# First pair's projection weights and first normalised tokens in small parts, and a transposed-probability copy moved between two low-part subtractions

## The chip, the cores and the metric

The kernel runs on one core of one Trainium2 chip. The metric is the device time of one execution in microseconds (us); lower is better. Three runs of the kernel before took 746.08, 747.19 and 747.55 us, median 747.19 us.

## The reference, cut to what matters

A decoder layer over x of shape (16, 128, 256), all in float32:

```
x = x + attn(layernorm(x), Wq, Wk, Wv, Wr)                     # 16 heads of 64, causal penalty -50
x = x + xattn(layernorm(x), ctx, ctx, w_q, w_k, w_v, w_o)      # 16 heads of 64, no mask
x = x + ffn(layernorm(x))                                      # shared SwiGLU + 8 experts, two chosen per token

attn:  q, k, v = x @ Wq, x @ Wk, x @ Wv                        # 256 -> 1024 columns each
       p = softmax(q k^T / 8 + mask);  out = (p v) @ Wr
```

## The kernel before, in words

**Precision.** A float32 matrix is split into a high part (rounded to the fast matmul type, by ScalarE) and a low part (the rest, by VectorE or GpSimd). `product` (L145 to L149) multiplies two such matrices in three matmuls: low by high, high by high, high by low, at L147, L148 and L149.

**Tiling.** The 2048 tokens are four groups of 512 (four sequences of 128). The 16 heads are eight pairs of two, so that a pair's q or k is a tile of 128 rows and 512 tokens. Two pairs make a duo; a group has four duos d = 0 to 3, self-attention has 16 duos and cross-attention 16 more, so that the attention is a pipeline of 32 duos. After it come the gating, the shared and the routed feed-forward. The order of every engine is written out by hand, and the engines meet at semaphores alone.

**A duo.** On TensorE (`duo` inside `attention_tensor`): the weighted values of the two pairs of the duo before last (`weighted_values`, L887, into the two banks of psW), the transposes of the first pair's probabilities of the duo before (`p_transposes(pe, 0)`, L873, into both banks of psT), the scores of this duo's two pairs (`scores`, L941, into psS and psA), the transposes of the second pair's probabilities (`p_transposes(pe, 1)`, again into psT), and then projections of q, k and v for what follows, and the output projection. In the last quarter of `scores(p, 1)` TensorE waits (`psT_free`) until both banks of psT have been copied out: bank 0 by ScalarE (`pT0_copy`, L580), bank 1 by VectorE (`pT1_copy`, L717). VectorE's order at the head of a duo is `oT_split_lo` of pair 0, `oT_split_lo` of pair 1 (L721: the low part of the weighted values, which needs ScalarE's high part, L584), then `pT1_copy`, then the row minima of the scores (L740). The output projection and the next user of each psW bank need the low parts.

**The start.** SP loads two of the first group's four token tiles (ScalarE's queue the other two) and then three weight pieces of 512 KB each, half the columns of Wq, Wk and Wv, into three slots of `stage` (`PIECES`, `load`). Every later piece waits until the piece in its slot has been split. TensorE runs 13 matmuls on the identity (`WARM`, L904), each of which shows as two records. VectorE takes the statistics and normalises the four tiles (L210); `first_z_transposes` (L243) transposes each tile into two banks, k = 1 and k = 0; ScalarE rounds each 512-token bank (`z_split_hi`, L251) and VectorE subtracts (`z_split_lo`, L257). ScalarE's order there is wq high (L337), z high, wk high, wv high; VectorE's is z rows, wq low (L341), z low, wk low, wv low. Then TensorE makes q and k of pair 0 (`q_or_k`), a quarter of v (`v_project`), the scores of pair 0 (`scores(0, 0)`), and q and k of pair 1.

Of the kernel before, what the change touches and what calls it, by code (L numbers as in the profile page):

```python
# [20 lines left out]
F32 = mybir.dt.float32  # L21
F32R = mybir.dt.float32r
ACT = mybir.ActivationFunctionType
# [3 lines left out]
P = 128  # L27
# [19 lines left out]
CHUNK = KT * INNER  # L47
WARM = 13
STAGES = 3
# [12 lines left out]
def build(nc, x, ctxT, wq, wk, wv, wr, xq, xk, xv, xr, w1, win, wout, w2, wgate, bgate, out):  # L62
    ctx = ExitStack()
    with ctx:
        def sem(name):
            return ctx.enter_context(nc.semaphore(name))
# [34 lines left out]
        rstd_seen, z_centred = sem("rstd_seen"), sem("z_centred")  # L101
        first_eps, first_rstd = sem("first_eps"), sem("first_rstd")
        zT_mm, z_hi, z_lo = sem("zT_mm"), sem("z_hi"), sem("z_lo")
        qk_mm, q_copied, k_copied = sem("qk_mm"), sem("q_copied"), sem("k_copied")
# [100 lines left out]

        def first_rows(dve):
            for half, known in ((FIRST, first_rstd), (SECOND, rstd_done)):
                dve.wait_ge(known, 1)
                for t in range(half.start, half.stop):
                    nc.vector.tensor_scalar(z[:, t, :], row_tile(0, t), mv[:, t, 0:1], rstd[:, t:t + 1],  # L210
                                            ALU.subtract, ALU.mult).then_inc(z_done, 1)
# [15 lines left out]
        Z_IN_S = ((1, psS[:, 0, :]), (0, psS[:, 1, :]))  # L227
        Z_FIRST = ((1, psW[:, 0, :]), (0, psT[:, 0, :]))
        Z_IN_A = ((1, psA[:, 0, :]), (0, psA[:, 1, :]))
# [8 lines left out]

        def first_z_transposes(pe, halves):
            for t in range(TPG):  # L240
                pe.wait_ge(z_done, t + 1)
                for k, bank in halves:
                    mm = nc.tensor.transpose(bank[:, t * P:(t + 1) * P], z[:, t, k * P:(k + 1) * P], ident[:])  # L243
                    if t == TPG - 1:
                        mm.then_inc(zT_mm, 1)

        def z_split_hi(act, g, halves, hi=None):
            hi = zhi if hi is None else hi
            for n, (k, bank) in enumerate(halves):
                act.wait_ge(zT_mm, g * KT + n + 1)  # L250
                nc.scalar.activation(hi[:, k, :], bank, ACT.Copy).then_inc(z_hi, 1)  # L251
# [43 lines left out]
        def token_half(pair, z_g, t, half, k):  # L295
# [12 lines left out]
        PIECES = [f"{w} {half}" for w, half in  # L308
                  (("wq", "lower"), ("wk", "lower"), ("wv", "lower"), ("wq", "upper"), ("wk", "upper"), ("wr", "lower"),
                   ("wv", "upper"), ("wr", "upper"),  # L310
# [74 lines left out]
        with att:  # L385
# [33 lines left out]
            pieces = [columns(Q, wq, lower, -SCALE), columns(K, wk, lower, 1.0), columns(V, wv, lower, 1.0),  # L419
                       columns(Q, wq, upper, -SCALE), columns(K, wk, upper, 1.0), pair_rows(wr, slice(0, HP)),  # L420
# [165 lines left out]
            def attention_scalar(act):  # L586
# [137 lines left out]
            def attention_vector(dve):  # L724
# [5 lines left out]
                def first_lo(n):  # L730
                    weights_lo(dve, n, pieces[n][2], pieces[n][1], pieces[n][3])
# [15 lines left out]
                def duo(G, d, after, causal=True, depth=2, sub=0):  # L747
# [152 lines left out]
            def attention_tensor(pe):  # L900
# [956 lines left out]
```

## Time and profile before

| | |
|---|---|
| three runs, us | 746.08, 747.19, 747.55 |
| profiled execution: its time, us | 745.39 |
| profiled execution: its span, us | 743.7 |
| granted TensorE clock, mean of the span | 1.000 |
| TensorE matmul busy | 735.5 us (99% of the span) |
| VectorE busy | 460.3 us (62%) |
| ScalarE busy | 443.2 us (60%) |
| GpSimd busy | 309.3 us (42%) |

The span runs from the first to the last instruction; the execution's own time is 1.7 us more. PE is TensorE's matmuls, PEld its weight loads, DVE VectorE, ACT ScalarE, POOL GpSimd, SPq and ACTq the DMA issues of these engines. L12 is a line of the kernel. Matmuls are pipelined, so that a record's duration overlaps the next record: what one takes of TensorE's time is read from start to start.

### The profile page before, as it was taken

The page shows a single profiled execution, that of the slowest core. Times are in us where ns is not written, and L with a number is a line of the kernel's source. Part 1 is how long each engine was busy: PE and PEld are TensorE (multiplying, and loading weights), DVE is VectorE, ACT ScalarE, POOL GpSimd, SP SyncE. Part 2 cuts the span into 40 slices and gives each one's busy share as a digit, 9 for nine tenths or more (in the row PEclk, how much of TensorE's full clock was granted, in tenths as well). Part 3 has the DMA queues.
Part 4 walks back from the last instruction along what each step waited for, and adds up shares of the span by engine and source line. Part 5 has one row for each costly group of instructions (what it writes and reads, how often), then busy time and mean ns, then how long its engine had stood idle before and what let it go on. Part 6 is the DMA issues. An engine that isn't in the chain of part 4 may idle for free.

```text
span 743.7 us, 17776 instructions
## 1 busy us (share of the span) xinstructions
PE 735.5 (99%) x6371; PEld 643.2 (86%) x6371; DVE 460.3 (62%) x947; ACT 443.2 (60%) x1469; POOL 309.3 (42%) x336
## 2 busy tenths in 40 slices
PE   7999999999999999999999999999999999999998
PEld 6888888888988888888888889888887889999987
DVE  6776677766766875554466456455777746444277
ACT  4876666666656678766566666657744534555322
POOL 2656225222523556463244236323760772555400
PEclk9999999999999999999999999999999999999999
DMA  7599800000000013000000000300150455767272
GB/s 235 175 372 192 263 1 0 0 0 0 0 0 0 30 37 107 2 26 5 1 0 28 0 0 1 112 0 2 30 226 1 185 200 179 240 207 213 69 270 67
DMA packets 35418, 64.68 MB, mean 87 GB/s; under 512 B 7940, under 2 KB 14596, under 8 KB 34788
## 3 DMA queue, kind: packets, MB, share of 16 engines
q1 hardware_dynamic: 30644, 50.17, 21.8%
q0 software_dynamic: 4432, 13.54, 4.8%
q8 instruction: 33, 0.54, 0.3%
q10 hardware_dynamic: 288, 0.26, 0.1%
q14 instruction: 21, 0.17, 0.1%
HBM read 38.06 MB, written 30.09 MB: 92 GB/s over the span
## 4 chain that ended last, share of the span: by engine, by line
PE 98%; ACT 1%; DVE 0%; POOL 0%; issue 0%; POOLq 0%; DVEq 0%
PE psW L147 15%; PE psW L149 14%; PE psW L148 14%; PE psW L887 8%; PE psT L873 5%; PE psT L147 4%; PE psT L148 4%; PE psT L149 4%; PE psA L941 4%; PE psS L941 4%; PE psS L147 4%; PE psS L148 3%; PE psS L149 3%; PE psA L149 2%; PE psA L148 2%; PE psA L147 2%
## 5 line engine op out<-in xcount | busy, mean ns | idle before, releaser
L506 POOL TENSOR_TENSOR prob<-prob,rsum 128x512 f32<-128x512 f32 x128 | 134.8, 1055 | 287.9 <-DVE rsum L745 287.8
L609 ACT ACTIVATE prob<-psA,nmin 128x128 f32<-128x128 f32 x256 | 91.8, 384 | 1.3
L609 ACT ACTIVATE prob<-psS,nmin 128x128 f32<-128x128 f32 x256 | 90.4, 376 | 1.9 <-DVE nmin L740 1.9
L584 ACT ACTIVATE oT_hi<-psW 128x512 fp32r<-128x512 f32 x63 | 37.7, 598 | 88.2 <-PE psW L887 88.2
L580 ACT ACTIVATE pT<-psT 128x512 f32<-128x512 f32 x64 | 38.3, 598 | 54.3 <-PE psT L873 53.4
L745 DVE RECIPROCAL rsum<-psums 128x4 f32<-128x4 f32 x128 | 21.9, 171 | 71.4 <-ACT prob L609 71.2
L721 DVE TENSOR_TENSOR oT_lo<-psW,oT_hi 128x512 fp32r<-128x512 f32 x63 | 43.5, 691 | 31.4 <-ACT oT_hi L584 31.0
L887 PE MATMUL psW<-pT,v 128*64 128x128 f32 x1008 | 62.3, 276 | 0.0
L728 DVE COPY kt<-psW 128x512 f32<-128x512 f32 x57 | 39.3, 689 | 36.7 <-PE psW L149 36.7
L887 PEld LDWEIGHTS psW<-pT,v 128*64 128x64 f32 x1008 | 54.4, 137 | 6.6 <-issue 3.1
L609 ACT ACTIVATION_READ_ACCUMULATOR prob<-psA,nmin 128x1 f32 x256 | 57.5, 225 | 0.0
L1241 POOL DMA_INDIRECT yt<-z,probs x39 | 37.9, 972 | 46.8 <-ACT z L1323 32.6
L609 ACT ACTIVATION_READ_ACCUMULATOR prob<-psS,nmin 128x1 f32 x256 | 55.6, 217 | 0.0
L147 PE MATMUL psW<-zlo,wq_hi 128*128 128x512 f32 x128 | 53.2, 416 | 1.4 <-DVE zlo L257 1.4
L149 PE MATMUL psW<-zhi,wq_lo 128*128 128x512 f32 x128 | 50.6, 395 | 0.0
L148 PE MATMUL psW<-zhi,wq_hi 128*128 128x512 f32 x128 | 50.3, 393 | 0.0
L595 ACT ACTIVATE q<-psW 128x512 f32<-128x512 f32 x64 | 38.9, 608 | 17.2 <-PE psW L149 16.9
L147 PE MATMUL psW<-wo_lo,oT_hi 128*128 128x256 f32 x168 | 48.9, 291 | 0.0
L148 PE MATMUL psW<-wo_hi,oT_hi 128*128 128x256 f32 x168 | 46.8, 279 | 0.0
L149 PE MATMUL psW<-wo_hi,oT_lo 128*128 128x256 f32 x168 | 46.8, 278 | 0.0
L873 PE MATMUL psT<-ident,prob 64*128 64x64 f32 x1024 | 44.9, 225 | 0.0
L873 PEld LDWEIGHTS psT<-ident,prob 64*128 64x128 f32 x1024 | 39.5, 139 | 5.8 <-issue 5.8
(378 smaller groups left out, 2194.7 us busy)
## 6 DMA issues: line engine op xcount, KB each, us to landing
stage<-hs SPq DMA_DIRECT2D x39, 257.0 KB, 2.9
hs<-empty SPq DMA_DIRECT2D x1, 9984.0 KB, 35.2
w_lo<-w_raw SPq DMA_DIRECT2D x4, 1024.0 KB, 8.1
w_hi<-yt SPq DMA_DIRECT2D x4, 1024.0 KB, 9.4
stage<-ctxT SPq DMA_DIRECT2D x4, 512.0 KB, 4.3
xres<-x SPq DMA_DIRECT2D x3, 512.0 KB, 6.9
out<-xres SPq DMA_DIRECT2D x12, 128.0 KB, 2.0
stage<-wq SPq DMA_DIRECT2D x2, 512.0 KB, 4.0
```

The source lines that it names most:

```text
L147: nc.tensor.matmul(o, lh, rl, start=start, stop=False, **kw)
L148: nc.tensor.matmul(o, lh, rh, start=False, stop=False, **kw)
L149: return nc.tensor.matmul(o, ll, rh, start=False, stop=stop, **kw)
L506: nc.gpsimd.tensor_tensor(prob[i][:, r, :], prob[i][:, r, :], rsum[i][:, r].unsqueeze(2).broadcast_to([P, TPG, P]), ALU.mult).then_inc(pro ...
L580: nc.scalar.activation(flat(pT[i][:, 0, :, :]), psT[:, 0, :], ACT.Copy).then_inc(pT0_copied, 1)
L595: nc.scalar.activation(q[i][:], psW[:, Q, :], ACT.Copy).then_inc(q_copied, 1)
L609: e = nc.scalar.activation(prob[i][:, n, :], flat(psX[i][:])[:, n * P:(n + 1) * P], ACT.Exp, bias=nmin[i][:, n:n + 1], scale=-1.0, accum_o ...
L721: nc.vector.tensor_tensor(flat(oT[i][1][:]), bank, flat(oT[i][0][:]).bitcast(F32), ALU.subtract).then_inc(oT_lo, 1)
L728: nc.vector.tensor_copy(kt[i][:], bank).then_inc(k_copied, 1)
L873: mm = nc.tensor.transpose(psT[:, half, c], prob[i][r, n, :], ident[r, r])
L887: mm = nc.tensor.matmul(bank[r, keys].rearrange("p (a q) -> p a q", a=2), v[:, b, c], pT[i][:, :, h * TPG + b, :], start=True, stop=True, ...
L941: mm = nc.tensor.matmul(psX[i][:, h, c], q[i][r, c], kt[i][r, c], start=True, stop=True, skip_group_check=True)
```

## The change

Four things change at the start, and one in every duo.

- The first pair's 128 columns of Wq and of Wk are pieces of their own (128 KB each), loaded ahead of all others into a spare part of `stage` and split with their own semaphores. The other 384 columns of each lower half follow after wv, and TensorE waits for them (`wk lower`) ahead of q and k of pair 1.
- The first z is transposed, rounded and subtracted by halves of 256 tokens: tokens of tiles 0 and 1 in psW and psT, tokens of tiles 2 and 3 in the two banks of psS. q of pair 0 is computed in two halves of 256 tokens, k of pair 0 in one.
- VectorE's low part of the first wq columns stands between the rows of tiles 0 and 1 and those of tiles 2 and 3.
- `WARM` is 10 instead of 13.
- In each duo that has all three, VectorE's `pT1_copy` stands between the two `oT_split_lo`.

```diff
-WARM = 13
+WARM = 10
-        def first_rows(dve):
+        def first_rows(dve, between):
             for half, known in ((FIRST, first_rstd), (SECOND, rstd_done)):
+                if half is SECOND:
+                    between()
-        Z_FIRST = ((1, psW[:, 0, :]), (0, psT[:, 0, :]))
+        Z_FIRST_A = ((1, psW[:, 0, :]), (0, psT[:, 0, :]))
+        Z_FIRST_B = ((1, psS[:, 0, :]), (0, psS[:, 1, :]))
+        TOKENS_A, TOKENS_B = slice(0, GT // 2), slice(GT // 2, GT)
...
+                for k, bank in Z_FIRST_A if t < TPG // 2 else Z_FIRST_B:
                     mm = nc.tensor.transpose(bank[:, t * P:(t + 1) * P], z[:, t, k * P:(k + 1) * P], ident[:])
+                    if t == TPG // 2 - 1:
+                        mm.then_inc(first_zT, 1)
...
+        def first_split_hi(act, halves, tokens, transposed, signal):
+            for n, (k, bank) in enumerate(halves):
+                act.wait_ge(transposed, n + 1)
+                nc.scalar.activation(zhi[:, k, tokens], bank[:, tokens], ACT.Copy).then_inc(signal, 1)
+
+        def first_split_lo(dve, halves, tokens, copied, signal):
+            for n, (k, bank) in enumerate(halves):
+                dve.wait_ge(copied, n + 1)
+                nc.vector.tensor_tensor(zlo[:, k, tokens], bank[:, tokens], zhi[:, k, tokens].bitcast(F32),
+                                        ALU.subtract).then_inc(signal, 1)
...
-                  (("wq", "lower"), ("wk", "lower"), ("wv", "lower"), ("wq", "upper"), ...
+                  (("wv", "lower"), ("wq", "lower"), ("wk", "lower"), ("wq", "upper"), ...
+            FIRST_PAIR, OTHER_PAIRS = slice(0, P), slice(P, HC)
+            first_pieces = [columns(Q, wq, FIRST_PAIR, -SCALE), columns(K, wk, FIRST_PAIR, 1.0)]
+            first_stage = [stage[:, n + 1, CHUNK // 2:CHUNK // 2 + KT * P].rearrange("p (a b) -> p a b", a=KT) for n in range(2)]
...
+                for n in range(2):
+                    sp.dma_start(first_stage[n], first_pieces[n][0]).then_inc(first_in[n], 16)
                 for n in range(STAGES):
                     load(sp, n, pieces[n][0])
...  (ScalarE)
-                first_hi(Q)
-                z_split_hi(act, 0, Z_FIRST)
-                first_hi(K)
-                first_hi(V)
+                first_pair_hi(Q)
+                first_split_hi(act, Z_FIRST_A, TOKENS_A, first_zT, first_z_hi)
+                first_split_hi(act, Z_FIRST_B, TOKENS_B, zT_mm, z_hi)
+                first_pair_hi(K)
+                first_hi(PIECES.index("wv lower"))
                 q_copy(0, 0)
+                first_hi(PIECES.index("wq lower"))
+                first_hi(PIECES.index("wk lower"))
                 v_copy(0, 0, 0, psT[:, 1, :])
...  (VectorE, in a duo)
                         oT_split_lo(dve, p - 4, 0, psW[:, 0, :])
-                        oT_split_lo(dve, p - 4, 1, psW[:, 1, :])
                     if depth > 0:
                         pT1_copy(dve, p - 2, 0)
+                    if depth > 1:
+                        oT_split_lo(dve, p - 4, 1, psW[:, 1, :])
...  (VectorE, the start)
-                first_rows(dve)
-                first_lo(Q)
-                z_split_lo(dve, 0, Z_FIRST)
-                first_lo(K)
-                first_lo(V)
+                first_rows(dve, lambda: first_pair_lo(Q))
+                first_split_lo(dve, Z_FIRST_A, TOKENS_A, first_z_hi, first_z_lo)
+                first_split_lo(dve, Z_FIRST_B, TOKENS_B, z_hi, z_lo)
+                first_pair_lo(K)
+                first_lo(PIECES.index("wv lower"))
                 k_copy(0, 0)
+                first_lo(PIECES.index("wq lower"))
+                first_lo(PIECES.index("wk lower"))
...  (TensorE)
-                first_z_transposes(pe, Z_FIRST)
-                q_or_k(0, Q, 0, None, 0)
-                q_or_k(0, K, 0, None, None)
+                first_z_transposes(pe)
+                pe.wait_ge(first_w_lo, 1)
+                first_product(Q, TOKENS_A, first_z_lo, True, False)
+                first_product(Q, TOKENS_B, z_lo, False, True)
+                pe.wait_ge(first_w_lo, 2)
+                first_product(K, slice(0, GT), None, True, True)
                 wait_lo(pe, "wv lower")
                 v_project(0, 0, 0, psT[:, 1, :])
                 scores(0, 0, free=False)
+                wait_lo(pe, "wk lower")
                 q_or_k(0, Q, 1, None, None)
```

`first_pair_hi(n)` and `first_pair_lo(n)` are one ScalarE and one VectorE instruction on 128x256 numbers, as L337 and L341 are on 128x1024. `first_product` is `product` for each k (1, then 0) on the tokens given, into psW, with a wait for each k's low part where `known` is given.

## Rows read from the trace of the kernel before

**Rows 1.** Page, part 4: share of the span in the chain that ended last.

```profile
PE 98%; ACT 1%; DVE 0%; POOL 0%; issue 0%; POOLq 0%; DVEq 0%
```

**Rows 2.** Waits of PE: waiting, releaser, us in total, times, longest.

```profile
PE psW L147 <- DVE zlo L257: 1.4, 1, 1.4
```

**Rows 3.** Timeline of PE, 2 to 8 us, then 6.95 to 7.45: start, us, what.

```profile
2.44 5.17 PE L904 MATMUL psA<-ident 128*128 128x128 f32 x26 [2.44 <-POOL mask L499]
...
6.78 0.83 PE L904 MATMUL psA<-ident 128*128 128x128 f32 x6
```

**Rows 4.** Timeline of all engines, 0 to 22 us.

```profile
6.40 1.06 ACT L337 ACTIVATE wq_hi<-stage 128x1024 fp32r<-128x1024 f32 x1 [3.39 <-DMA stage<-wq]
6.72 0.75 DVE L210 TENSOR_SCALAR z<-xres,mv,rstd 128x256 f32<-128x256 f32 x2 [0.27 <-POOL rstd L193]
...
8.41 0.60 ACT L251 ACTIVATE zhi<-psW 128x512 fp32r<-128x512 f32 x1 [0.96 <-PE psW L243]
...
10.48 1.23 DVE L341 SCALAR_TENSOR_TENSOR wk_lo<-stage,wk_hi 128x1024 fp32r<-128x1024 f32 x1
...
11.76 0.50 PE L147 MATMUL psW<-zlo,wk_hi 128*128 128x512 f32 x1 [0.25 <-DVE wk_lo L341]
...
13.26 0.39 PE L147 MATMUL psT<-wv_lo,zhi 128*128 128x512 f32 x1
...
15.84 0.50 PE L147 MATMUL psW<-zlo,wq_hi 128*128 128x512 f32 x1
...
21.10 1.11 ACT L337 ACTIVATE wq_hi<-stage 128x1024 fp32r<-128x1024 f32 x1
```

**Rows 5.** DMA issues between 1.6 and 2.75 us: KB each, us from issue to landing.

```profile
stage<-wq SPq DMA_DIRECT2D x1, 512.0 KB, 4.7
xres<-x SPq DMA_DIRECT2D x1, 128.0 KB, 3.0
...
stage<-wv SPq DMA_DIRECT2D x1, 512.0 KB, 6.3
```

**Rows 6.** Timeline of PE in a duo of the middle, 306 to 309.4 us.

```profile
307.67 1.14 PE L941 MATMUL psA<-kt,q 64*128 64x128 f32 x16
308.61 0.69 PE L873 MATMUL psT<-ident,prob 64*128 64x64 f32 x16
309.23 0.50 PE L147 MATMUL psW<-zlo,wq_hi 128*128 128x512 f32 x1
```

**Rows 7.** Timeline of DVE in the same duo.

```profile
306.04 0.69 DVE L721 TENSOR_TENSOR oT_lo<-psW,oT_hi 128x512 fp32r<-128x512 f32 x1 [0.97 <-ACT oT_hi L584]
306.92 0.69 DVE L721 TENSOR_TENSOR oT_lo<-psW,oT_hi 128x512 fp32r<-128x512 f32 x1 [0.18 <-ACT oT_hi L584]
307.53 0.68 DVE L717 COPY pT<-psT 128x512 f32<-128x512 f32 x1
```

**Rows 8.** Timeline of PEld there, 308.305 to 308.31 us: the one load in flight.

```profile
308.28 0.18 PEld L941 LDWEIGHTS psA<-kt,q 64*128 64x128 f32 x1
```

**Rows 9.** Timeline of ACT there.

```profile
306.92 0.60 ACT L580 ACTIVATE pT<-psT 128x512 f32<-128x512 f32 x1
...
310.92 0.60 ACT L595 ACTIVATE q<-psW 128x512 f32<-128x512 f32 x1 [0.33 <-PE psW L149]
```

**Rows 10.** Timelines of PE and DVE in the second duo, 27 to 30.2 us.

```profile
28.57 1.06 PE L941 MATMUL psA<-kt,q 64*128 64x128 f32 x16
29.46 0.66 PE L873 MATMUL psT<-ident,prob 64*128 64x64 f32 x16
30.05 0.50 PE L147 MATMUL psW<-zlo,wq_hi 128*128 128x512 f32 x1
...
27.85 0.69 DVE L717 COPY pT<-psT 128x512 f32<-128x512 f32 x1
```

**Rows 11.** Timeline of PE, third and last duo: the block in psA.

```profile
42.19 1.12 PE L941 MATMUL psA<-kt,q 64*128 64x128 f32 x16
...
521.63 1.14 PE L941 MATMUL psA<-kt,q 64*128 64x128 f32 x16
```

More of the change, by code:

```diff
@@ L102, in build @@
         first_eps, first_rstd = sem("first_eps"), sem("first_rstd")
+        first_in = [sem(f"first_in{n}") for n in range(2)]
+        first_w_hi, first_w_lo = sem("first_w_hi"), sem("first_w_lo")
+        first_zT, first_z_hi, first_z_lo = sem("first_zT"), sem("first_z_hi"), sem("first_z_lo")
         zT_mm, z_hi, z_lo = sem("zT_mm"), sem("z_hi"), sem("z_lo")
@@ L237, in z_transposes, with first_z_transposes @@
                 mm.then_inc(zT_mm, 1)
-        def first_z_transposes(pe, halves):
+        def first_z_transposes(pe):
             for t in range(TPG):
                 pe.wait_ge(z_done, t + 1)
-                for k, bank in halves:
+                for k, bank in Z_FIRST_A if t < TPG // 2 else Z_FIRST_B:
                     mm = nc.tensor.transpose(bank[:, t * P:(t + 1) * P], z[:, t, k * P:(k + 1) * P], ident[:])
+                    if t == TPG // 2 - 1:
+                        mm.then_inc(first_zT, 1)
                     if t == TPG - 1:
                         mm.then_inc(zT_mm, 1)
+        def first_split_hi(act, halves, tokens, transposed, signal):
[7 more added lines that the diff above has]
+                                        ALU.subtract).then_inc(signal, 1)
         def z_split_hi(act, g, halves, hi=None):
@@ L308, in build @@
         PIECES = [f"{w} {half}" for w, half in
-                  (("wq", "lower"), ("wk", "lower"), ("wv", "lower"), ("wq", "upper"), ("wk", "upper"), ("wr", "lower"),
+                  (("wv", "lower"), ("wq", "lower"), ("wk", "lower"), ("wq", "upper"), ("wk", "upper"), ("wr", "lower"),
                    ("wv", "upper"), ("wr", "upper"),
@@ L417, in pair_rows @@
                 return (k_rows(src)[:, r, :], wo_hi[:, r, :], wo_lo[:, r, :], 1.0)
-            pieces = [columns(Q, wq, lower, -SCALE), columns(K, wk, lower, 1.0), columns(V, wv, lower, 1.0),
+            FIRST_PAIR, OTHER_PAIRS = slice(0, P), slice(P, HC)
+            first_pieces = [columns(Q, wq, FIRST_PAIR, -SCALE), columns(K, wk, FIRST_PAIR, 1.0)]
+            first_stage = [stage[:, n + 1, CHUNK // 2:CHUNK // 2 + KT * P].rearrange("p (a b) -> p a b", a=KT) for n in range(2)]
+            pieces = [columns(V, wv, lower, 1.0), columns(Q, wq, OTHER_PAIRS, -SCALE), columns(K, wk, OTHER_PAIRS, 1.0),
                        columns(Q, wq, upper, -SCALE), columns(K, wk, upper, 1.0), pair_rows(wr, slice(0, HP)),
@@ L684, in first_hi, with first_pair_hi @@
                     weights_hi(act, n, pieces[n][1], pieces[n][3])
-                first_hi(Q)
-                z_split_hi(act, 0, Z_FIRST)
-                first_hi(K)
-                first_hi(V)
+                def first_pair_hi(n):
+                    act.wait_ge(first_in[n], 16)
+                    nc.scalar.activation(first_pieces[n][1], first_stage[n], ACT.Copy,
+                                         scale=first_pieces[n][3]).then_inc(first_w_hi, 1)
+                first_pair_hi(Q)
[3 more added lines that the diff above has]
+                first_hi(PIECES.index("wv lower"))
                 q_copy(0, 0)
+                first_hi(PIECES.index("wq lower"))
+                first_hi(PIECES.index("wk lower"))
                 v_copy(0, 0, 0, psT[:, 1, :])
@@ L840, in attention_vector, with first_pair_lo @@
                 first_stats(dve)
-                first_rows(dve)
-                first_lo(Q)
-                z_split_lo(dve, 0, Z_FIRST)
-                first_lo(K)
-                first_lo(V)
+                def first_pair_lo(n):
+                    dve.wait_ge(first_w_hi, n + 1)
+                    nc.vector.scalar_tensor_tensor(first_pieces[n][2], first_stage[n], first_pieces[n][3],
+                                                   first_pieces[n][1].bitcast(F32), ALU.mult, ALU.subtract).then_inc(first_w_lo, 1)
+                first_rows(dve, lambda: first_pair_lo(Q))
[3 more added lines that the diff above has]
+                first_lo(PIECES.index("wv lower"))
                 k_copy(0, 0)
+                first_lo(PIECES.index("wq lower"))
+                first_lo(PIECES.index("wk lower"))
                 for d in range(PEEL):
@@ L1046, in duo, with first_product @@
                             projections(1, True, first_copied)
-                first_z_transposes(pe, Z_FIRST)
-                q_or_k(0, Q, 0, None, 0)
-                q_or_k(0, K, 0, None, None)
+                def first_product(n, tokens, known, start, stop):
+                    for i, k in enumerate((1, 0)):
+                        if known is not None:
+                            pe.wait_ge(known, i + 1)
+                        mm = product(psW[:, n, tokens], (wh[n][:, k, FIRST_PAIR], wl[n][:, k, FIRST_PAIR]),
+                                     (zhi[:, k, tokens], zlo[:, k, tokens]), start and i == 0, stop and i == KT - 1,
+                                     skip_group_check=True)
+                    if stop:
+                        mm.then_inc(qk_mm, 1)
+                first_z_transposes(pe)
[4 more added lines that the diff above has]
+                first_product(K, slice(0, GT), None, True, True)
                 wait_lo(pe, "wv lower")
```

## The prediction

> **What bounds the kernel now.** I read the chain of waits first: 98% of the span is TensorE's work [rows 1]. So two questions are left: where TensorE stands still, and where its work is slower than it need be. The table of waits answers the first for the large stops: 1.4 us ahead of q's first matmul, for the low part of z, and at 11.76 us a short one of 0.25 for the low part of wk; it names none in a duo [rows 2, 4]. The start's timeline then shows what TensorE is fed by: the transposes wait behind the warm-up, ScalarE takes the two banks of z and then wk, VectorE the low parts one after another [rows 3, 4]. For stops too short for the table I compared the same piece of TensorE's program from start to start in two duos. In the second duo, scores in psA to next transposes to q's first matmul take 29.46 - 28.57 = 0.89 and 30.05 - 29.46 = 0.59 us, together 1.48 [rows 10]. In a middle duo the same instructions take 0.94 and 0.62, together 1.56 [rows 6]. The matmul rows name no cause, the weight loads do: in the middle duo the load for the last quarter of the scores starts at 308.28 [rows 8], 0.07 after VectorE's copy of psT's second bank ends (307.53 + 0.68 = 308.21) [rows 7], and TensorE waits for this very copy there (`psT_free`). In the second duo that copy ended at 28.54, before the scores began [rows 10]. So TensorE does wait in a steady duo, by 0.05 us; the other 0.03 comes in the transposes behind it, which I read as the two heads' records running out of step after the stop. Of 32 such blocks the first two lie ahead of the pattern; the third to the last are 30, and their own durations (1.12 and 1.14 against 1.06) carry its mark at both ends [rows 10, 11].
>
> **The reordered copy.** It removes nothing and adds nothing; it puts `pT1_copy` ahead of the second low part. VectorE is free at 306.04 + 0.61 = 306.65 (two such instructions in a row start 0.61 apart [rows 7]), and psT is ready when ScalarE's copy of the other bank starts, 306.92 [rows 9]. The copy then runs 306.92 to 307.60, and ScalarE's ends at 307.52, both well ahead of 308.22, where the load would come unhindered. The stop goes. Per duo 1.56 - 1.48 = 0.08 us, by 30 duos 2.3 us; I take 2.2, as the third duo's stop is smaller. The ends: nothing, if the stop is something else; 30 x 0.08 = 2.4 at the most. What is late next: the second low part, now 307.53 to 308.22, is wanted by TensorE only in the projections behind q, whose six matmuls start at 309.23, so more than 2 us later [rows 6]; it is covered by the scores in psA, the transposes and q. The row minima queued behind it start at the same time as before, since the two instructions have only changed places, and the 0.18 us that VectorE idled for ScalarE now goes into waiting for the transposes [rows 7]. ScalarE is fed by TensorE again right after (0.33 us idle before the copy of q at 310.92 [rows 9]), so its work moves forward with TensorE's and doesn't hold the gain back. I price these at zero.
>
> **The start.** I follow the new order with rows' durations. Where the trace has no such size (128x256) I take 0.45 us on ScalarE and 0.42 on VectorE, estimates: z's rows of that size take (0.75 us for two that overlap, so 0.34 apart) [rows 4], and 128x512 takes 0.60 on ScalarE, 0.69 on VectorE [rows 4, 7]. Back to back I space them 0.34. Upper end: no gain over the 512 size, 0.60.
> - Warm-up: 26 records from 2.44 to 7.45, the last six 0.11 apart from 6.78, so the 20 before took 4.34 us, 0.217 each [rows 3]. Ten matmuls are these 20: the warm-up ends at 6.78, which is where the spacing falls to its fast value, the level of 2.4 GHz against 1.2. The transposes of tiles 0 and 1 (their rows are done before) follow at 6.78 to 7.22.
> - wq's first columns (128 KB, issued at 1.70 like wq before): between 3.0 us, as a token tile of this size, and 4.7, as the whole wq [rows 5], so landed between 4.7 and 6.4; I take 4.9, the nearer size. ScalarE's high part then lies beside the statistics, and VectorE's low part in the 0.27 us in which it idled before 6.72 [rows 4]: it starts at 6.45, the second rows 0.34 later at 6.79, which is 0.07 late, ending 7.54. Landed at 6.4, they would be 0.45 late.
> - z's high parts on ScalarE: 7.30, 7.64, and for the second half (transposes from 7.63) 7.98, 8.32 to 8.77. Low parts on VectorE: 7.78, 8.12, 8.46, 8.80 to 9.22. TensorE computes q in between; its last three short matmuls end at about 9.67. The high part of wk's first columns starts at 8.66, the low part at 9.14 to 9.57.
> - k: six matmuls from 9.67, ready for v at 11.1 (before: 11.76 to 13.26, 1.50 with its slow first one [rows 4]).
> - wv: high part 9.00 to 10.06 on ScalarE, low part 10.09 to 11.31 on VectorE (1.06 and 1.23 for this size [rows 4]). v starts at 11.36, 0.25 us after TensorE is free: this is the wait that takes the place of the 1.4. wv was issued at 2.69 and took 6.3 [rows 5], landed 8.99; now 256 KB stand ahead of it instead of 1 MB, so it should be there. Were it to land with the old delay it would just do.
> - v and the scores of pair 0 take what they took, 15.84 - 13.26 = 2.58 [rows 4]: TensorE is at pair 1 at 13.94. Its new wait there, for wk's other columns: VectorE copies k at 11.45 to 12.14, then two low parts of 128x768 (0.96 each, 1.23 x 3/4 and a little, spaced 0.88) to 13.90. Just in time, 13.95. Behind this wait q and k of pair 1 are queued and everything else of TensorE; behind VectorE's two low parts stands the mask of the first scores, which come at 14.0.
> So pair 1 starts at 13.95 instead of 15.84: 1.9 us. With 0.60 for each small ScalarE step (five of them ahead of wv, each 0.15 dearer, and the last low part behind) v starts at 12.1, and the gain is 1.1; with a ScalarE step of 0.38 it is 2.2. The later slots of `stage`: the upper wq is now issued after wv's low part at 11.3, and ScalarE takes it at 21.10 - 1.9 = 19.2 [rows 4], 7.9 us later, where pieces of its size landed in 4.7 to 6.3 [rows 5]. Hidden, and without that cover it would cost what the landing is late. SP's two added issues push its later ones back by some half a microsecond each, the pieces of wq, wk and the gate's weights among them; their cover is the 2 us between their landing (like wv's before, about 9.0) and their first use at 10.9 on ScalarE.
>
> **A rule of the skill against it.** The rise of TensorE's spacing comes at 6.6 to 6.8 us in this execution, with no reserve for a shorter warm-up [rows 3]. The Trainium skill ("TensorE: Matmul & The Clock Gate", section "What's actually happening") says that the array is throttled until activity releases it, and that how many matmuls run slow differs between runs of one kernel. By that rule some executions would enter q and k at half the clock. One trace can't show the spread; I make it the third case below.
>
> **Sum.** 745.39 - 1.9 - 2.2 = 741.3 us for the profiled execution; the runs' median lies 1.80 above that execution, so 743.1 for the runs.
>
> **Rivals.**
> A. *Both steps as above*: 743.1, own range 742.1 to 744.3 (start 1.1 to 2.2, duos 1.8 to 2.4, and half a microsecond of scatter, as the three runs show).
> B. *The duos give nothing.* For: 0.05 us is at the edge of what start times tell, and another wait, as ScalarE's copy of q before the output projection, could swallow it. Against: load and copy end keep 0.07 between them, and the second duo runs the same program without it. 747.19 - 1.9 = 745.3.
> C. *The start gives nothing, by the clock.* With the warm-up gone from 6.78 on, the pauses between the small q products leave TensorE less active than before, and the spacing stays at 0.217 per 128 two-pass columns until about 12. q's 12 short matmuls and k's 6 then cost twice 0.115 and twice 0.23, 1.4 us more each where they are not waiting; k would end at some 13.3, as before. 747.19 - 2.2 = 745.0.
> D. *Slower than before.* The same mechanism, lasting: with the low clock from 9.7 us on, each microsecond so spent costs half of one, all of it on the path. To eat 4.1 us it must last 8.2 us, to 18; to 24 it costs 7.1 against 4.1 won, 750.2. For: TensorE pauses more in this start than now. Against: it has no pause over 0.5 us from 8.2 on, while the old one paused 1.4 us before q [rows 2] and was fast after it (six matmuls of k in 1.50 [rows 4]).
> E. *No change*: both B and C, 747.2.
>
> **Chances.** A 0.68, B 0.12, C 0.14, D 0.03, E 0.03. The range for 8 in 10 reaches from 741.7 to 745.6, A with both its ends and the centres of B and C. About 0.2% (1.5 us) is what a measurement of this kernel can tell: faster means below 745.7. A lies there whole, B by some 0.6 of its cases, C by 0.75: 0.68 + 0.07 + 0.10 = 0.85. Same 0.12, slower 0.03.
>
> **What would show it.** Right: the psA block and its transposes take 1.48 us from start to start in all duos, and the weight load no longer follows VectorE's copy by 0.07; pair 1's q starts near 14.0; wv's low part ends at 11.3 and v starts right behind; warm-up records end at 6.8 with transposes 0.11 apart. Wrong: matmuls of k some 0.46 us apart (C, D); ScalarE idle for wv or for wq's first columns past 5 us (the pieces land late); a block still at 1.56 with the load behind another instruction's end (B); q of pair 1 later than 14.5 behind wk's low part.

## The result, and the profile after

The changed kernel took 741.66 us (median of six runs, 741.35 to 741.98); the kernel before, now in six runs, 747.26 us (746.08 to 748.93). The ratio is 0.9925, 95% interval 0.9913 to 0.9937: 5.6 us faster, where 4.1 was forecast, and 0.04 us below the range. The two profiled executions stand closer to the forecast than the medians do: 745.39 and 741.35 us, 4.04 apart, spans 743.7 and 739.6. So the reading falls into two parts: what the traces show of the 4.1 us, and where the other 1.5 are.

**The duos.** Timeline of PE in the same middle duo of the changed kernel (start, us, what), to be read against [rows 6]:

```profile
304.78 1.06 PE L981 MATMUL psA<-kt,q 64*128 64x128 f32 x16
305.67 0.66 PE L913 MATMUL psT<-ident,prob 64*128 64x64 f32 x16
306.26 0.50 PE L150 MATMUL psW<-zlo,wq_hi 128*128 128x512 f32 x1
```

and of DVE, against [rows 7]:

```profile
303.16 0.69 DVE L753 TENSOR_TENSOR oT_lo<-psW,oT_hi 128x512 fp32r<-128x512 f32 x1 [0.97 <-ACT oT_hi L608]
304.06 0.69 DVE L749 COPY pT<-psT 128x512 f32<-128x512 f32 x1 [0.21 <-PE psT L913]
304.67 0.68 DVE L753 TENSOR_TENSOR oT_lo<-psW,oT_hi 128x512 fp32r<-128x512 f32 x1
```

Scores to q take 306.26 - 304.78 = 1.48 us, as in the second duo of before [rows 10], instead of 1.56, and the row's own duration is 1.06 instead of 1.14. The copy ends at 304.75, before TensorE's block in psA starts. VectorE's idle time has moved from the low part to the copy, as forecast. From pair 1's q to the last scores before took 522.50 - 15.84 = 506.66 us and after 518.32 - 14.31 = 504.01: 2.65 us for 30 duos.

**The start.** PE, ACT and DVE of the changed kernel, to be read against [rows 3, 4]:

```profile
2.44 4.63 PE L944 MATMUL psA<-ident 128*128 128x128 f32 x20 [2.44 <-POOL mask L523]
...
5.33 0.42 ACT L712 ACTIVATE wq_hi<-stage 128x256 fp32r<-128x256 f32 x1 [2.33 <-DMA stage<-wq]
...
6.20 0.42 DVE L876 SCALAR_TENSOR_TENSOR wq_lo<-stage,wq_hi 128x256 fp32r<-128x256 f32 x1
...
6.87 0.42 PE L250 MATMUL psW<-ident,z 128*128 128x128 f32 x1
7.08 0.42 PE L250 MATMUL psT<-ident,z 128*128 128x128 f32 x1
...
7.75 0.38 ACT L259 ACTIVATE zhi<-psW 128x256 fp32r<-128x256 f32 x1 [2.01 <-PE psW L250]
...
8.74 0.36 PE L150 MATMUL psW<-zlo,wq_hi 128*128 128x256 f32 x1 [0.31 <-DVE zlo L264]
...
10.31 1.22 DVE L361 SCALAR_TENSOR_TENSOR wv_lo<-stage,wv_hi 128x1024 fp32r<-128x1024 f32 x1 [0.39 <-ACT wv_hi L357]
...
13.30 0.95 DVE L361 SCALAR_TENSOR_TENSOR wk_lo<-stage,wk_hi 128x768 fp32r<-128x768 f32 x1
...
14.31 0.50 PE L150 MATMUL psW<-zlo,wq_hi 128*128 128x512 f32 x1
```

The chain is the one that was written down, 0.36 us later at its end: pair 1's q at 14.31 for 13.95, against 15.84 before. The delay comes in at one place. The first transposes are 0.21 us apart, not 0.11: TensorE was still at its lower clock, as rival C had it, but for one microsecond only (the granted clock rose at 7.94 us, in the first trace of before at 6.67). From there everything is late: z's high part at 7.75 (7.30 forecast), wv's low part ends at 11.53 (11.31), wk's other columns at 14.25 (13.90).

Behind the last scores both traces take nearly the same time (221.16 and 221.26 us, to the end of the span). 1.53 + 2.65 - 0.10 = 4.08: the traces are accounted for.

### The profile page after: what moved, and what is told of

Same layout as the page of the kernel before. It is cut to its first block, busy times and chain, and to the rows that moved or that the text cites. A ratio compares the mean times of both kernels' runs of the same rounds, so it can differ in the third digit from the quotient of the medians.

```text
span 739.6 us, 17762 instructions
## 1 busy us (share of the span) xinstructions
PE 732.7 (99%) x6371; PEld 641.1 (87%) x6371; DVE 459.8 (62%) x951; ACT 443.6 (60%) x1473; POOL 309.3 (42%) x336
## 4 chain that ended last, share of the span: by engine, by line
PE 98%; ACT 0%; DVE 0%; POOL 0%; issue 0%; POOLq 0%; DVEq 0%
PE psW L150 15%; PE psW L152 14%; PE psW L151 14%; PE psW L927 8%; PE psT L913 5%; PE psT L150 4%; PE psT L152 4%; PE psT L151 4%; PE psS L981 4%; PE psA L981 4%; PE psS L150 4%; PE psS L152 3%; PE psS L151 3%; PE psA L152 2%; PE psA L151 2%; PE psA L150 2%
## 5 line engine op out<-in xcount | busy, mean ns | idle before, releaser
L150 PE MATMUL psW<-zlo,wq_hi 128*128 128x512 f32 (+1 forms) x130 | 53.5, 412 | 0.3 <-DVE zlo L264 0.3
L152 PE MATMUL psW<-zhi,wq_lo 128*128 128x512 f32 (+1 forms) x130 | 50.8, 391 | 0.0
L151 PE MATMUL psW<-zhi,wq_hi 128*128 128x512 f32 (+1 forms) x130 | 50.6, 389 | 0.0
L749 DVE COPY pT<-psT 128x512 f32<-128x512 f32 x64 | 43.9, 685 | 6.6 <-PE psT L913 6.4
L772 DVE TENSOR_REDUCE nmin<-psA 128x4 f32<-128x512 f32 x64 | 43.9, 687 | 1.1
```

Source lines behind the costliest of these rows:

```text
L150: nc.tensor.matmul(o, lh, rl, start=start, stop=False, **kw)
L151: nc.tensor.matmul(o, lh, rh, start=False, stop=False, **kw)
L152: return nc.tensor.matmul(o, ll, rh, start=False, stop=stop, **kw)
L749: nc.vector.tensor_copy(flat(pT[i][:, 1, :, :]), psT[:, 1, :]).then_inc(pT1_copied, 1)
L772: nc.vector.tensor_reduce(nmin[i][:, h * TPG:(h + 1) * TPG], sc, AX.X, ALU.min).then_inc(min_done, 1)
```

## The experiments

Kernels of one batch ran on one chip with runs of the kernel before beside them. In three of the four batches every kernel, the one before too, has a stop of some 19 us near 600 us (below), so that times are compared within a batch. Its length differs from execution to execution: behind the last scores the twelve traces with the stop take 238.7 to 241.1 us, the six without it 221.1 to 221.4. So batches 1, 2 and 4 carry up to 2.4 us of scatter that no part of this change makes.

**Batch 1: the parts alone.** Before was at 766.50 us there.

E1, the reorder alone (the diff's part in the duos, put into the kernel before). 

> The kernel before with one edit: in each duo VectorE's copy of the transposes stands between the two low parts. Theory T1 (the duos' stops are all that the reorder takes, 30 x 0.08 us, and what the runs moved beyond the traces' 4.1 us belongs to them, as their length differs from run to run): median 3.5 to 4.0 us under before, runs within 0.7 us of each other as the changed kernel's are. Rival T2 (the part beyond 4.1 us belongs to the start): 2.2 to 2.4 us under before, runs scattered over 1.5 to 3 us as before's. Rival T3 (the part beyond is only that the profiled execution of before was an unusually quick one): 2.4 us under before whatever the scatter. Trace: score block and transposes 1.48 us from start to start in every duo.

 Measured: 763.73 us (760.64 to 765.48), ratio 0.9964 (0.9949 to 0.9978), 2.8 us less (1.7 to 3.9 by the interval, so that this run alone doesn't tell T1 from T2 and T3). Trace: 305.75 to 307.23 from scores to q, 1.48 us.

E2, the start alone:

```diff
                         oT_split_lo(dve, p - 4, 0, psW[:, 0, :])
+                        oT_split_lo(dve, p - 4, 1, psW[:, 1, :])
                     if depth > 0:
                         pT1_copy(dve, p - 2, 0)
-                    if depth > 1:
-                        oT_split_lo(dve, p - 4, 1, psW[:, 1, :])
```

> The changed kernel with the old order in the duos: the low parts first, then the copy. T1: 1.5 us under before (pair 1's q at 14.3 instead of 15.8 us), runs as scattered as before's. T2: 3 us under before, runs tight. T3: 1.6 us under before. Trace: the stop is back, 1.56 us from start to start in every duo, the weight load 0.07 us behind the copy's end.

 Measured: 763.36 us (761.87 to 766.02), ratio 0.9962 (0.9949 to 0.9975), 2.9 us less. Trace: q of pair 1 at 14.03; the stop is back (1.56 us from scores to q in the steady duos).

The parts add up (0.9964 x 0.9962 = 0.9926, the whole change 0.9925). The reorder gives what its trace says. The start gives 2.9 us, nearly twice what the first pair of traces says, though its interval reaches down to 1.9: T1, which gave the missing part to the duos, fell, and T2 stands, save that its other sign failed: neither kernel's runs drew together here (E2's reach over 4.2 us). The stop near 600 us hides part of what that sign could show.

E3, the kernel before again. 

> The kernel before, unchanged, for a second trace of it: what differs between two executions of the same program. T1: time within 0.2% of before's median; if this execution is longer than 745.39 us, the excess stands in the duos, as longer stops in the last quarter of the scores in psA. T2: the excess stands ahead of pair 1's q (15.84 us in the first trace), as a later rise of TensorE's spacing. T3: no excess, some 745.4 us.

 Measured: 765.57 us (764.87 to 768.40), ratio 0.9991 (0.9978 to 1.0005). Trace: pair 1's q at 15.79, so no excess at the start; but from there to the last scores 507.72 us instead of 506.66. The 1.05 us stand in the cross-attention loop's output projection. Timeline of PE and ACT in one of its duos, the first execution of before:

```profile
366.65 0.62 ACT L595 ACTIVATE q<-psW 128x512 f32<-128x512 f32 x1
...
367.39 0.32 PE L147 MATMUL psW<-wo_lo,oT_hi 128*128 128x256 f32 x1
...
368.79 0.28 PE L147 MATMUL psT<-wo_lo,oT_hi 128*128 128x256 f32 x1
```

and in the second, with PEld's row:

```profile
366.82 0.62 ACT L595 ACTIVATE q<-psW 128x512 f32<-128x512 f32 x1
...
367.49 0.19 PEld L147 LDWEIGHTS psW<-wo_lo,oT_hi 128*128 128x128 f32 x1 [0.21 <-ACT q L595]
...
367.55 0.32 PE L147 MATMUL psW<-wo_lo,oT_hi 128*128 128x256 f32 x1
...
369.01 0.28 PE L147 MATMUL psT<-wo_lo,oT_hi 128*128 128x256 f32 x1
```

The weight load follows the end of ScalarE's copy of q (367.44) by 0.05 us, and the block takes 1.40 us in the one execution and 1.46 in the other, in all ten duos of the loop's inside; the block behind it 1.45 and 1.50. The loop settles into one of two rhythms and keeps it. But the wait is not what differs. In both executions the load starts 0.05 us behind the copy's end, and the first matmul's step is 0.156 and 0.162 us; each of the 22 steps behind it takes 0.1134 us in the one and 0.1177 in the other, at the full granted clock in both. What spaces them differently isn't shown.

The rhythm has to be kept apart when the duos are priced. From pair 1's q to the last scores, with the old order in the duos, three traces in the short rhythm take 506.9 us on average (first, E10, E16) and four in the long one 507.7 (E2, E3, E11, E14); with the new order 504.0 in two (first, E5) and 504.8 in four (E1, E4, E12, E13). In either rhythm the reordered copy is worth 2.9 us, as E1's runs have it.

E4, 13 warm-up matmuls in the changed kernel (`WARM = 13`). 

> The changed kernel with 13 warm-up matmuls instead of 10. If the clock rises by the time since the first matmul, as before (6.7 us), the 6 more records cost 0.11 each and the transposes of tiles 0 and 1 come at 7.45 with fast spacing, tiles 2 and 3 right behind: pair 1's q within 0.2 us of the changed kernel's 14.31. If the rise comes at a time that changes from execution to execution, whatever the warm-up, then records up to it are 0.21 apart and the transposes start at 7.45 to 8.0: up to 0.5 us slower. Time against the changed kernel: 0 to +0.5 us.

 Measured: 762.38 us (761.39 to 763.49), ratio 0.9949 (0.9932 to 0.9967); the changed kernel's own ratio is 0.9923 to 0.9925, so it is slower than that by some 2 us, with intervals that overlap, where at most 0.5 was expected. Trace: q of pair 1 at 14.84, 0.5 us later than with 10; it is also in the long rhythm. The shorter warm-up is worth half a microsecond in the trace, and no trace shows the loss that it risked.

**Batch 2: other orders.** Before was at 765.97 us.

E5, the changed kernel again. 

> The changed kernel, unchanged, beside the kernel before on this chip. Theory T1 (the traces are right, duos 2.7 us and start 1.5 us; the rest of the 5.6 us is scatter of the kernel before alone): 4.0 to 4.5 us under before. Rival T4 (the kernel before really loses 1.5 us more in most executions than in its profiled one, and the changed kernel doesn't): 5.2 to 6 us under before again, and its own runs within 1 us.

 Measured: 760.34 us (760.07 to 760.82), ratio 0.9923 (0.991 to 0.9937): 5.6 us again. T4 stands: the kernel before is usually slower than its profiled execution, the changed one isn't.

E6, ScalarE's copy of q one exponential earlier:

```diff
-                        exps(p, 1, range(2, 6 if depth > 1 else 4))
+                        exps(p, 1, range(2, 5 if depth > 1 else 4))
                         q_copy(p + 2, 1)
-                        exps(p, 1, range(6 if depth > 1 else 4, 8))
+                        exps(p, 1, range(5 if depth > 1 else 4, 8))
```

> The changed kernel with ScalarE's copy of the second pair's q (of the next duo) one exponential earlier in duos 1 and 2. In the changed kernel's trace the weight load of the output projection starts 0.05 us after that copy ends, in 22 duos, where its twelve matmuls take 1.44 to 1.46 us against 12 x 0.115 = 1.38. If that wait is real: 1.3 to 2 us under the changed kernel, the block at 1.38. If the 0.06 is only the change of tile shape: no change within 0.3 us.

 Measured: 757.97 us (757.71 to 759.57), ratio to before 0.9897 (0.988 to 0.9913), 2.4 us under the changed kernel (1.3 to 2 were expected). The same two rows, 1.37 us apart and without the longer first one:

```profile
362.51 0.28 PE L150 MATMUL psW<-wo_lo,oT_hi 128*128 128x256 f32 x1
...
363.88 0.28 PE L150 MATMUL psT<-wo_lo,oT_hi 128*128 128x256 f32 x1
```

The wait was real: the first step is 0.113 us instead of 0.156. The long rhythm doesn't show either: all twelve blocks from the loop on take 1.36 us, with steps of 0.1134, here and in the two other traces with this edit (E9, E15).

E7, the second low part later still:

```diff
-                    if depth > 1:
-                        oT_split_lo(dve, p - 4, 1, psW[:, 1, :])
                     minima(p, 0, 0, causal)
                     minima(p, 0, 1, causal)
+                    if depth > 1:
+                        oT_split_lo(dve, p - 4, 1, psW[:, 1, :])
```

> The changed kernel with the second low part behind both row minima, 1.3 us later again. If the low part has the 2 us of cover that the prediction gave it: same time as the changed kernel within 0.5 us. If TensorE's projections behind q wait for it: up to 1.3 us a duo, 30 us in all.

 Measured: 771.01 us (770.01 to 772.19), ratio 1.0056 (1.004 to 1.0071): 10.7 us over the changed kernel. PE's waits:

```profile
PE psW L150 <- DVE oT_lo L753: 6.6, 14, 0.5
```

The expected 1.3 us was wrong: the low part now ends 3.0 us later in a masked duo (the mask doubles what stands ahead of it), and TensorE waits for it in 14 duos, 0.5 us each by the table. From start to start such a duo loses 0.73 us, 10.2 in all. The 16 duos of cross-attention, where the low part comes 1.5 us later, take 246.8 us against 245.9, and the 0.9 is no more than the long rhythm, in which this trace is. So the cover was there as the prediction had it: in the changed kernel's trace the low part ends at 74.70 and the first projection that wants it starts at 77.09, 2.4 us.

E8, the copy behind both low parts and the first minima. 

> The changed kernel with VectorE's copy of the transposes behind both low parts and behind the first row minima. If TensorE waits for the end of this copy alone, each of the 30 duos loses what the copy comes later beyond the moment it is wanted: 0.6 us later than in the kernel before, in 14 unmasked duos (one instruction of minima), 1.3 in 15 masked ones (mask and minima): 26 to 32 us over the changed kernel. If something else ends the wait: under 5 us.

 Measured: 802.17 us (two runs), ratio 1.0467: 41.8 us over the changed kernel. Timelines of an unmasked duo, PE and DVE:

```profile
385.97 0.49 PE L983 MATMUL psA<-kt,q 64*128 64x128 f32 x4 [0.75 <-issue]
...
384.58 0.69 DVE L772 TENSOR_REDUCE nmin<-psS 128x4 f32<-128x512 f32 x1 [0.25 <-PE psS L983]
385.19 0.68 DVE L749 COPY pT<-psT 128x512 f32<-128x512 f32 x1
```

The last quarter of the scores starts at 385.97, 0.10 after the copy's end at 385.87. TensorE's wait for this instruction is shown. My size (26 to 32) was short by a third: I left out that the minima can't start before the scores in psS are done (the 0.25 us of idle time), so that the block takes 1.88 us unmasked and 2.62 masked, for 0.89.

**Batch 3: the kernel before's own scatter.** Before was at 747.69 us (22 runs, 746.47 to 749.85), without the stop at 600.

E9, the same earlier copy of q in the kernel before. 

> The kernel before with ScalarE's copy of q one exponential earlier in duos 1 and 2, nothing else. Theory T5 (in the cross-attention loop the wait of the output projection for this copy settles into one of two lengths, 1.40 or 1.46 us for its block and 1.45 or 1.50 for the next, 1.05 us over the loop; the kernel before is mostly in the long one, the changed kernel in the short one, and its first profiled execution was in the short one): the wait goes, so the gain over before is the 22 waits and the 1.05 us, 2.5 to 3.5 us, and the runs draw together. Without T5 the gain is as over the changed kernel, 2 to 2.5 us, and the scatter stays.

 Measured: 745.62 us (744.85 to 746.72), ratio 0.9967 (0.9957 to 0.9978), 2.1 us less, under the 2.5 that T5 asked for. All blocks of the loop at 1.36 us again; the runs reach over 1.9 us for 3.4, with half as many of them. In its trace wq's first piece is split only at 7.56:

```profile
7.56 1.06 ACT L337 ACTIVATE wq_hi<-stage 128x1024 fp32r<-128x1024 f32 x1 [4.55 <-DMA stage<-wq]
...
9.02 0.60 ACT L251 ACTIVATE zhi<-psW 128x512 fp32r<-128x512 f32 x1 [0.40 <-PE psW L243]
...
16.43 0.50 PE L147 MATMUL psW<-zlo,wq_hi 128*128 128x512 f32 x1
```

E10, 10 warm-up matmuls in the kernel before (`WARM = 10`). 

> The kernel before with 10 warm-up matmuls instead of 13. The transposes of the first z then start near 7.5 us, where the last rows are ready, instead of 7.45 to 8.0. T1 and T5: pair 1's q at 15.6 to 15.9 as before, time within 0.5 us of before, unless the order of events at the start moves the loop into its other length, 1 us less. Rival T6 (the warm-up is what the start's gain comes from): 1 to 1.5 us under before.

 Measured: 748.41 us (745.11 to 750.69), ratio 1.0009 (0.9996 to 1.0022). T6 fell: the shorter warm-up alone gives nothing, though q of pair 1 is at 15.27 in its trace, earlier than the 15.6 expected.

E11, before a third time. 

> The kernel before once more, for a third trace. T5: output-projection blocks in the cross-attention loop at 1.46 us (long), as in the second trace. If it is at 1.40, the long one is not what most executions show, and T5 doesn't explain before's median.

 Measured: 749.71 us, one run, near the upper end of the batch; its trace holds a term that the first one doesn't show. ACT and PE, then the table of stretches (busy time and instructions of PE, PEld, DVE, ACT and POOL, granted clock, DMA share, GB/s):

```profile
8.54 1.06 ACT L337 ACTIVATE wq_hi<-stage 128x1024 fp32r<-128x1024 f32 x1 [5.54 <-DMA stage<-wq]
...
11.61 0.47 PE L147 MATMUL psW<-zlo,wq_hi 128*128 128x512 f32 x1 [3.42 <-DVE zlo L257]
...
18.69 0.50 PE L147 MATMUL psW<-zlo,wq_hi 128*128 128x512 f32 x1
```

```profile
10.00:12.00 2.00, 0.39 (x2) 0.38 (x3) 2.00 (x4) 2.00 (x4) 0.00 (x0) 1.00 0.06 16
...
13.00:16.00 3.00, 3.00 (x9) 2.18 (x8) 1.33 (x2) 0.60 (x1) 0.00 (x0) 0.50 0.71 254
```

The first 512 KB piece of wq landed 6.8 us after its issue, not 4.7. ScalarE's high parts of z are queued behind that of wq, so TensorE stood idle for 3.4 us, up to 11.61; 1.2 us after that its granted clock fell to the lower level, and k took 2.73 us instead of 1.50. Pair 1's q started 2.85 us later than in the first trace: 1.72 of it stand ahead of q's first matmul, the other 1.13 behind it, where the clock was low. The loop's rhythm was the long one.

E12, the changed kernel a third time. 

> The changed kernel once more, for a third trace. T5: output-projection blocks in the cross-attention loop at 1.40 us (short), as in the first two; pair 1's q at 14.0 to 14.5.

 Measured: 742.23 us. Pair 1's q at 14.32, but the loop is in the long rhythm. So the rhythm isn't tied to the change: of T5 only the two lengths are left, not that the changed kernel keeps the short one.

**Batch 4: landing or idle clock.** Before was at 764.31 us (762.61 to 767.50).

E13, the small pieces with z whole:

```diff
-                first_split_hi(act, Z_FIRST_A, TOKENS_A, first_zT, first_z_hi)
-                first_split_hi(act, Z_FIRST_B, TOKENS_B, zT_mm, z_hi)
+                z_split_hi(act, 0, Z_FIRST)
...
-                first_product(Q, TOKENS_A, first_z_lo, True, False)
-                first_product(Q, TOKENS_B, z_lo, False, True)
+                first_product(Q, slice(0, GT), z_lo, True, True)
```

and the same for the transposes and VectorE. 

> The changed kernel with the first z whole again (two banks of 512 tokens, one product for q), the small first pieces kept. Theory T8 (before's runs lose what the trace doesn't show because the first 512 KB piece lands between 4.7 and 6.8 us after its issue and everything of the start hangs on it; the small pieces land by 3.8 and have room): nearly all of the start's gain stays, 4.5 to 5.3 us under before, runs within 1 us; the halves are worth only the 0.5 to 1 us that is left. Rival T9 (the halves fill TensorE's idle time and so keep its clock up, and that draws the runs together): 3 to 4 us under before, runs scattered over 2 us or more.

 Measured: 759.41 us (758.80 to 762.42), ratio 0.9934 (0.9914 to 0.9953), 4.9 us less. Trace: q of pair 1 at 15.27. Of the whole change's 5.6 us the halves are worth some 0.7 by the medians (within both intervals) and 0.96 by the traces; the small pieces carry the rest of the start. The gain is as T8 has it, the scatter isn't: these six runs reach over 3.6 us, which is T9's sign. The stop near 600 us scatters by up to 2.4 of it, so that the sign settles nothing. What speaks for T8 is a pair of traces. E10, with the whole first piece landed after 4.7 us, and E13, with the small one, both with 10 warm-up matmuls, have pair 1's q at the same 15.27. With a quick landing the small piece wins nothing, while the medians give it some 2 us (4.9 less the 2.8 of E1; the intervals allow 1 us either way).

E14, before with TensorE's idle time filled:

```diff
                 first_z_transposes(pe, Z_FIRST)
+                for _ in range(5):
+                    nc.tensor.matmul(psA[:, 0, 0:P], ident[:], ident[:], start=True, stop=True)
```

> The kernel before with five more matmuls on the identity behind the first transposes of z, in TensorE's idle time ahead of q (1.4 us; they take 1.1 us at the fast clock). T8: no gain, same median and same scatter within 0.3 us. T9: the clock doesn't fall any more at 12.85 us as in before's third trace; the slow runs at 749 to 750 us go, the median falls by 0.5 to 1 us.

 Measured: 764.62 us (762.53 to 766.76), ratio 1.0003 (0.9989 to 1.0017). The idle time ahead of q is down to 0.3 us in its trace (a landing after 5.1 us) and nothing is won, and the runs are as scattered. So filling the 1.4 us of idle time is not what the change gains by. Whether TensorE kept busy through a late landing would keep its clock isn't tested: five such matmuls take 1.1 us, and the idle times there are 2.5 and 3.4 us.

E15, the better version again. 

> The changed kernel with ScalarE's copy of q one exponential earlier, for its time beside before on this chip: 7.5 to 8.5 us under before, 2 to 2.5 under the changed kernel's 741.7 if before is at 747.3.

 Measured: 758.13 us (756.73 to 759.06), ratio 0.9911 (0.9891 to 0.9931): 6.2 us under before, short of the 7.5 expected. With E6's 0.9897 it beats both kernels; the interval here is wider than the difference to the changed kernel, which E6 has beside it in its own batch.

E16, before a fourth time. 

> The kernel before, for a fourth trace. T8: pair 1's q starts the later the later the first piece of wq lands, near 15.8 us for a landing by 6.6 us and 1 us later for each us beyond that. T9: its start follows the clock's rise and fall alone.

 Measured: 767.27 us. The DMA issues of its first microseconds (KB each, us from issue to landing), and its timeline:

```profile
stage<-wq SPq DMA_DIRECT2D x1, 512.0 KB, 6.6
```

```profile
8.36 1.06 ACT L337 ACTIVATE wq_hi<-stage 128x1024 fp32r<-128x1024 f32 x1 [5.35 <-DMA stage<-wq]
...
18.27 0.50 PE L147 MATMUL psW<-zlo,wq_hi 128*128 128x512 f32 x1
```

The clock fell again, from 11.05 to 14.46. The four traces of the unchanged kernel and the two others that share its start, in order of landing:

| trace | wq first split at | q of pair 1 |
|---|---|---|
| before, first | 6.40 | 15.84 |
| before, second (E3) | 6.54 | 15.79 |
| E1 | 6.60 | 15.38 |
| E9 | 7.56 | 16.43 |
| before, fourth (E16) | 8.36 | 18.27 |
| before, third (E11) | 8.54 | 18.69 |

The order is not all the landing's doing. In E9 TensorE's clock rose only at 7.94: the transposes of z ended late, and ScalarE, done with wq, waited 0.40 us for them (its row above); the landing cost 0.14 us there, at VectorE's low part of z. E1 is early because the clock rose at 5.4. In the last two the landing does bind: z's high part stands right behind wq's, q's first matmul starts 1.54 and 1.72 us later than in the first trace, for a landing 1.96 and 2.14 us later, and the fallen clock adds 0.89 and 1.13 up to pair 1's q. In the eight traces with the new start the 128 KB piece was split between 4.73 and 5.68 us, VectorE wants it at 6.2, and q of pair 1 started between 13.73 and 14.48.

## Why the prediction was wrong where it was, and right where it was

**The bound** was read rightly, and so was the stop too short for the table of waits: removed (E1), put back (E2), lengthened (E8). The term "30 x 0.08, I take 2.2" measured 2.65 in the first pair of traces and 2.9 between traces of the same rhythm, above its own upper end, "2.4 at the most"; 46 ns a duo in the scores and 33 in the transposes make 2.4, and where the rest lies isn't shown.

**The start** was right as a mechanism, each wait in its place (0.3 us ahead of q, v behind wv's low part, pair 1 just behind wk's). "So pair 1 starts at 13.95 instead of 15.84: 1.9 us" measured 1.53 for the executions compared, by the late clock. That the sum for the profiled execution, 741.3, met its 741.35 us is luck: the start gave 0.4 us less and the duos 0.4 more.

**The step that failed is the sum**: "the runs' median lies 1.80 above that execution, so 743.1 for the runs". I carried the 1.80 over to the changed kernel as if it were scatter of the chip. The changed kernel's median lies 0.31 above its profiled execution (0.27 in E5's batch): most of the 1.80 belonged to the kernel before, and to the luck of its profiled execution, which was shorter than all six runs. What the traces show behind it is two executions of six with a late landing (E11, E16). They alone make up the 0.89 us by which the six traces with the old start average over the 15.84: 16.73 us for pair 1's q, for 14.16 in the eight with the new one, 2.57 us apart instead of 1.53. With the duos' 2.9 that makes 5.5 of the 5.6 us.

That sum is not as firm as it looks. The six traces reach over 3.3 us, so that their mean is uncertain by some 0.6 (an estimate from their scatter), and E11 and E16 were both near the upper end of their batches. By the middle of the traces instead of the mean (16.14 and 14.25) the start gives 1.9 us, and 0.8 us of the 5.6 stay open. How often the piece lands late, and whether the runs in the middle of the kernel before lose by it or by the long rhythm (1.05 us, in both kernels), these runs can't tell.

The page of before held the hint, and I used it for the new piece only: a DMA's landing taken from one execution is one draw. For the new small piece I bounded it from 4.7 to 6.4; for the old one that bound the whole start, I took one row as fixed. A bound on it could have come from the neighbours, 5.5 and 6.3 us for pieces of its own size. The range of rival A has a slip besides: its upper end, 744.3, leaves out the half microsecond of scatter that its lower end has.

**The rivals.** B was settled against by E1, E2 and E8. C came true for one microsecond of the changed kernel's start, and its cost was 0.36 us: the rise of the granted clock came anywhere between 5.3 and 8.1 us in eighteen executions. What I had not seen is that the clock speaks more against the kernel before: only there did it fall back within the start, in two traces of six, once within an idle time of 2.5 us and once 1.2 us after the end of one of 3.4. The Trainium skill's rule, that the array is throttled unless activity releases it and that the moment differs between runs ("TensorE: Matmul & The Clock Gate", "What's actually happening"), agrees with these traces. D and E had nothing. The chance of 0.85 for faster was placed rightly.

## What to carry to other kernels

A profile is one execution: when the runs scatter by more than the term you compute, ask which landing or clock state on the critical chain was a lucky draw, above all a large first transfer on which everything hangs, and price the edit by what it does to the other draws too. A small first piece, cut to what the first product needs, gains less in a good trace than in the median. If the program has two rhythms, compare only traces in the same one.

Stops of 0.05 us that no table of waits shows can be found by laying the same block of two iterations side by side and looking whose end the delayed weight load follows.

## What the runs showed of the hardware

- The same 512 KB load, issued at the same moment, landed 4.7, 4.7, 4.8, 4.9, 5.1, 5.8, 6.6 or 6.8 us after its issue in the eight executions that have it; a 128 KB one in its place took 3.0 to 4.0 in ten.
- TensorE's granted clock fell to half at 12.85 us in E11, 1.2 us after the end of an idle time of 3.4, and at 11.05 in E16, 2.1 us into one of 2.5; it was back at 16.27 and 14.46. In between k's six matmuls took 2.73 us in E11 instead of 1.50. After idle times of 1.4 to 1.7 us, in six other traces, it did not fall.
- The same matmuls of the output projection, at the full granted clock, started 0.1134 us apart in some executions and 0.1177 in others, each time for ten duos on end and in both kernels. In the three traces in which ScalarE's copy stood one exponential earlier (0.35 us) they were 0.1134 apart. The cause isn't shown.
- In three of four batches ScalarE, VectorE and TensorE stood idle for long stretches between 599 and 620 us while GpSimd issued indirect DMAs, and TensorE's clock fell. The part behind the last scores took 17 to 20 us longer there, in both kernels, and differently in each execution. It biases no comparison within a batch as far as the traces show, but it widens them. Its cause was not looked into.
